# The S products of a row tile whole, in the second half of the down bank, and programs of their own for the end

## Chip, cores and metric

One core of a Trainium2 chip. The metric is the device time of one launch in microseconds (us). Engines: TensorE (PE; its weight loads PEld), VectorE (DVE), ScalarE (ACT), GpSimd (POOL), SyncE (SP, which issues the DMAs).

## What is computed

x has 4 batches of 2048 tokens of 256 features, fp32. Each token is normalised (xn). One branch is a linear attention with L2-normalised queries and keys, the other a feed-forward of 704 hidden features whose inputs, hidden values and weights are rounded to FP4 in blocks of 16:

```python
xn = _layernorm(x)
Q, K, V = xn @ Wq.T + bq, xn @ Wk.T + bk, xn @ Wv.T + bv
Q, K = l2_norm(Q) (over the tokens), l2_norm(K)
tailor_sum = 1 / (L + Q . (sum(K) + EPS))
s = xn + gamma * (sum(V) + Q @ (K^T V)) * tailor_sum
h = silu(fp4_linear(xn, w_gate)) * fp4_linear(xn, w_up)
g = silu(fp4_linear(h, w_down))
out = x + s * g
```

As Q and K are linear in xn, the kernel gets s of a token from one 256x256 matrix per batch: s = xn @ M. M comes from the Gram matrix of the batch's tokens, by small products, so it is known only after the whole batch was normalised.

## The kernel before, in words

The 8192 tokens are 32 pairs (PAIRS) of two row tiles (j = 0 and 1) of 128 tokens, 8 pairs a batch (PB). One pass p of `iteration` works on many pairs at once, each engine with its own program and its order written out by hand; semaphores (S[...]) count what is done. Passes 0 to 11 are written out, 12 to 27 are a loop of two rounds with 8 passes each (`drive`), 28 to 32 are written out again, then each engine has a tail.

In pass p: pair p+3 is normalised and p+2 rounded (x_..., VectorE L917 to L942, ScalarE, GpSimd L495 to L512), pair p has its gate and up products (`gate_up`, L1427, two column halves c into the banks GU[:, c, 0..1]), silu on ScalarE (L635) and their product h on VectorE (`h_mul`, L953); pair p-1 has its hidden values rounded (VectorE `h_scales` L960 to L967, `h_round` L990, L993, L1001, GpSimd L546, ScalarE L684); pair p-2 has its hidden values transposed (`hidden_transposes`, L1389, copied by ScalarE L642, L644) and multiplied by w_down (`down_product`, L1437, L1439, into DS[:, 0:256], "D's bank"), and ScalarE makes g of it (`g_out`, L671). Pair e = p-10 (LAGE) has its S product, xn @ M (`s_terms`, L1448: 6 matmuls, high and low parts in f16), which VectorE scales by unm and multiplies by g into y. GpSimd adds x for pair p-12 (L562) and SyncE writes it out and loads the x of a later one (xe).

A gate or up bank has 512 columns, of which 352 are used. The S product of a row tile stands as two halves of 128 columns in the spare columns of the up banks:

```python
def s_spare(c, m=1):
    return GU[:, c, m, CH:CH + P]
```

A pass begins on VectorE with `h_mul` (0, 0), right behind L967 of the pass before. `s_half` follows each gate-up product, `e_half` (L1012) reads it right behind `h_mul`, and for the bank's sake gate_up waits for y_d and h_mul for s_d. `s_place` says which row tile it is: in j = 1 the first one of pair p-10, in j = 0 the second one of pair p-11. Passes 10 to 31 have them in this way. `last_halves`: in one pass a batch (step i = FIRST, j = 0) both halves stand together, since the next matrix M is due then.

The attention's small products are asked of TensorE at places of a table (`ASKS`, (step i, j, place)), answered by VectorE (`ANSWERS`) and copied by ScalarE (`COPIES`), step by step: Gram matrix (L1497), turn (L1506), t1q and t1k (L1512, L1519), squares and norms (L1527), raw (L1534), tailor (L1544; VectorE L1060), product (L1551), top (L1556), high_low (L1561; VectorE L1093, L1095 write M). The last batch has its own tables (`..._END`).

The end: the 8 pairs of the last batch can only have their S product when M of that batch is there. They use whole banks of 256 columns (`s_product`, read by `e_mul`, L1024), and y has two places, so e_mul waits for o_d of GpSimd's add two pairs back. x of the last 7 pairs is loaded early into buffers that have become free (xend); GpSimd adds into these (L557).

## Time and profile before

| | us |
|---|---|
| three runs, median (lowest to highest) | 596.38 (595.67 to 596.96) |
| the profiled execution, its time | 597.39 |
| its span, first to last instruction | 595.3 |
| PE busy | 549.7 (92%) |
| DVE busy | 555.4 (93%) |
| ACT busy | 416.8 (70%) |
| POOL busy | 265.6 (45%) |

The mean granted clock of TensorE was 0.991 of full speed. All times of rows are of the one profiled execution and count from its first instruction. A row's duration reaches to the end of the instruction's drain; the next one of the same engine can start some 0.1 to 0.16 us before that, so what an instruction holds of its engine is the distance from its start to the next start. "x2" is two instructions merged into one row. In brackets stands the idle time ahead and what ended it.

### The profile page before, as it was taken

What the parts mean: (1) busy time and instruction counts of PE and PEld (TensorE: products, weight loads), DVE (VectorE), ACT (ScalarE), POOL (GpSimd) and SP (SyncE); (2) the same over time, 40 slices, a digit from 0 to 9 for tenths busy, and PEclk for the clock granted to TensorE, in tenths of its full rate; (3) what the DMA queues carried; (4) which work ended last, traced back from release to release, by engine and by line L of the source; (5) the groups of instructions that cost most, each with busy time, mean ns of one, the idle gap of its engine ahead of it and who ended that gap; (6) DMA issues with size and microseconds to landing.
All of it is one profiled execution on the core that took longest, in us unless ns stands there. A gap on an engine that the chain in (4) does not pass through costs nothing. (4 is left out here: it accounts for less than half of the span.)

```text
span 595.3 us, 15174 instructions
## 1 busy us (share of the span) xinstructions
PE 549.7 (92%) x4957; PEld 426.7 (72%) x4957; DVE 555.4 (93%) x1178; ACT 416.8 (70%) x901; POOL 265.6 (45%) x214
## 2 busy tenths in 40 slices
PE   0478999999999999999999989999999999999896
PEld 0355767777787777777887757778787777778775
DVE  7998999999999999999999998999999999977763
ACT  4979878877778777776777667877776776654421
POOL 7533333333433555355544453354743453423226
PEclk9999999999999999999999989999999999999999
DMA  8010000000011001111110111111011111132033
GB/s 251 18 37 19 19 20 19 19 20 19 19 37 37 19 3 55 55 55 55 55 55 2 54 58 55 56 55 54 2 55 55 55 37 37 36 103 95 0 124 143
DMA packets 17488, 29.14 MB, mean 49 GB/s; under 512 B 2688, under 2 KB 4864, under 8 KB 17408
## 3 DMA queue, kind: packets, MB, share of 16 engines
q1 hardware_dynamic: 17408, 28.13, 14.4%
q8 instruction: 44, 0.72, 0.5%
q14 instruction: 36, 0.29, 0.2%
HBM read 19.73 MB, written 8.39 MB: 47 GB/s over the span
## 5 line engine op out<-in xcount | busy, mean ns | idle before, releaser
L1427 PE MATMUL GU<-wgu,xqT 128*128 128x352 f16 x1536 | 252.8, 315 | 4.1 <-DVE h L953 2.6
L1427 PEld LDWEIGHTS GU<-wgu,xqT 128*128 128x128 f16 x1536 | 148.5, 99 | 78.3 <-issue 4.1
L546 POOL TENSOR_TENSOR ht<-h,hrr 128x1408 f32<-128x1408 f32 x32 | 82.9, 2590 | 80.5 <-DVE hrr L967 79.0
L635 ACT ACTIVATE sil<-GU,wkap 128x352 f32<-128x352 f32 x128 | 71.0, 555 | 60.0 <-PE GU L1427 59.1
L1437 PE MATMUL DS<-wdT,hqT 128*128 128x256 f16 x704 | 88.4, 275 | 1.9 <-ACT hqT L642 1.9
L953 DVE SCALAR_TENSOR_TENSOR h<-GU,wkap,sil 128x352 f32<-128x352 f32 x128 | 69.1, 540 | 11.9 <-ACT sil L635 8.0
L1001 DVE TENSOR_TENSOR hq<-hg,hs 128x704 f16<-128x704 f16 x128 | 79.1, 659 | 1.0
L1437 PEld LDWEIGHTS DS<-wdT,hqT 128*128 128x128 f16 x704 | 67.3, 99 | 12.5 <-ACT hqT L642 2.3
L505 POOL TENSOR_TENSOR xnat<-xs,xnat 128x510 f16<-128x510 f32 (+1 forms) x32 | 37.0, 1158 | 85.3 <-DVE hq L1001 72.9
L495 POOL TENSOR_TENSOR rs<-ve,half 128x2 f32<-128x2 f32 x32 | 22.9, 717 | 112.2 <-DVE ht L990 106.5
L671 ACT ACTIVATE gring<-DS,hun 128x256 f32<-128x256 f32 (+1 forms) x64 | 30.0, 468 | 44.9 <-issue 30.9
L642 ACT COPY hqT<-TR 128x768 f16<-128x768 f16 x64 | 51.0, 796 | 9.0 <-PE TR L1389 8.1
L990 DVE SCALAR_TENSOR_TENSOR ht<-hT,ht 128x1408 f32<-128x1408 f32 x32 | 51.8, 1620 | 1.5 <-ACT hT L684 1.5
L1439 PE MATMUL DS<-wdT,hqT 128*128 128x256 f16 x384 | 52.4, 273 | 0.0
L993 DVE SCALAR_TENSOR_TENSOR hg<-hT,ht 128x1408 f16<-128x1408 f32 x32 | 51.8, 1620 | 0.0
L960 DVE TENSOR_REDUCE ham<-h 128x88 f32<-128x1408 f32 x32 | 51.4, 1608 | 0.0
L1389 PE MATMUL TR<-id,hq 128*128 128x128 f16 x704 | 49.7, 219 | 0.0
L1448 PE MATMUL GU<-Mx,xnT 128*128 128x128 f16 (+1 forms) x552 | 47.7, 222 | 1.7 <-DVE Mx L1095 1.7
L1448 PEld LDWEIGHTS GU<-Mx,xnT 128*128 (+1 forms) x552 | 39.3, 98 | 12.1 <-issue 1.9
L512 POOL TENSOR_TENSOR xt<-xs,xrr 128x512 f32<-128x512 f32 x32 | 34.0, 1062 | 27.1 <-DVE hq L1001 25.2
L684 ACT ACTIVATE hT<-ht 128x1408 f32<-128x1408 f32 x32 | 43.9, 1371 | 1.8 <-POOL ht L546 1.3
L644 ACT COPY hqT<-TR 128x640 f16<-128x640 f16 x64 | 45.1, 705 | 0.0
(166 smaller groups left out, 975.5 us busy)
## 6 DMA issues: line engine op xcount, KB each, us to landing
xin<-in_L_attn_x SPq DMA_DIRECT2D x34, 256.0 KB, 2.9
xe<-in_L_attn_x SPq DMA_DIRECT2D x25, 256.0 KB, 2.8
out<-o SPq DMA_DIRECT2D x25, 256.0 KB, 2.0
algebra<-in_L_ffn_w_down SPq DMA_DIRECT2D x1, 704.0 KB, 6.2
gring<-in_L_ffn_w_up SPq DMA_DIRECT2D x1, 640.0 KB, 4.8
xs<-in_L_attn_x SPq DMA_DIRECT2D x2, 256.0 KB, 4.2
xt<-in_L_attn_x SPq DMA_DIRECT2D x2, 256.0 KB, 4.7
out<-xin SPq DMA_DIRECT2D x2, 256.0 KB, 4.1
```

Source lines behind the costliest of these rows:

```text
L546: g.tensor_tensor(paired(ht[:, 0:2 * I]), paired(h[:, q]), spread(hrr[:, q], 4 * CB), ALU.mult).then_inc(S["ht_d"], 1)
L635: a.activation(sil[:, c], GU[:, c, 0, 0:CH], ACT.Silu, scale=wkap[:, 0:1]).then_inc(S["sil_d"], 1)
L642: a.copy(hqT[:, j, 0:6], TR[:, j, 0:6 * P].rearrange("p (c m) -> p c m", m=P)).then_inc(S["hA_ev"], 1)
L953: v.scalar_tensor_tensor(h[:, k, (2 * j + c) * CH:(2 * j + c + 1) * CH], GU[:, c, 1, 0:CH], wkap[:, 0:1], sil[:, c], ALU.mult, ALU.mult).t ...
L960: v.tensor_reduce(per_block(ham[:, :]), paired_in_order(h[:, q]), AX.X, ALU.max, apply_absolute_value=True).then_inc(S["ham_d"], 1)
L990: v.scalar_tensor_tensor(ht[:, 0:2 * I], hT[:, 0:2 * I], CUT, ht[:, 0:2 * I], ALU.max, ALU.subtract).then_inc(S["hw_d"], 1)
L993: v.scalar_tensor_tensor(hg[:, 0:2 * I], hT[:, 0:2 * I], CUT, ht[:, 0:2 * I], ALU.max, ALU.subtract).then_inc(S["hg_d"], 1)
L1001: v.tensor_tensor(paired(hq[:, q, j, at:at + I]), paired(hg[:, j * I:(j + 1) * I]), spread(scales[:, q, j * HB:(j + 1) * HB], HB), ALU.mul ...
L1427: last = t.matmul(GU[:, c, m, 0:CH], xqT[:, k, j, 2 * a_ + kc], wgu[:, b_, kc, 2 * m + c], start=(z == 0 and kc == 0), stop=(z == 2 and kc ...
L1437: t.matmul(DS[:, 0:D], hqT[:, j, z], wdT[:, z], start=(z == 0), stop=False)
L1439: last = t.matmul(DS[:, 0:D], hqT[:, j, LOCH + z], wdT[:, NCH + z], start=False, stop=(z == LOCH))
L1448: last = t.matmul(bank, slot[:, j, 2 * a_ + kc], Mb[:, b_, kc, columns], start=(i == 0 and kc == 0), stop=(i == 2 and kc == KD - 1))
```

## The change

- The S product of a row tile (except `last_halves` and the last pair of halves, in the tail) is one of 256 columns (`s_wide`) into DS[:, 256:512], the second half of D's bank. TensorE makes it at the start of `down_product`, which first waits until the last one is read (y_d).
- VectorE reads it in one instruction (`e_wide`) that also waits for g_d of the same pass and row tile, that is, until ScalarE has read D of it. For j = 0 it stands ahead of the first instruction of `h_round`, for j = 1 behind the last of `h_round` and ahead of `h_scales` (L960). The waits of gate_up on y_d and of h_mul on s_d go (but in one place a batch).
- Answers: gram1 moves behind the first half of the layernorm statistics, high_low ahead of L917.
- t1k uses the symmetry of the Gram matrix: 6 products of 128 columns in place of 4 of 256; ScalarE writes a doubled copy of a part of wkT once (`wkT_twice`).
- The end: pass 32 on TensorE and VectorE is a program of its own, which mixes product, top and high_low with the S products of pairs 21 to 23, the down products and the rounding. Each y of the last 8 pairs has its own place (in h, ht, y[:, 0]; the last one in G, in PSUM), and e_mul waits for no add of the pairs before but in one place. x of pair 24 is loaded into h. GpSimd waits for the last rounding ahead of the add of pair 22. The last pair's add is on VectorE in two halves (`o_last`), each with a DMA of its own.

Cut to its core (left out: tables of semaphores, the same edits in SyncE's and GpSimd's programs, ScalarE's copy):

```diff
-        ANSWERS = {(0, 0, 3): "gram0", (1, 0, 1): "gram1", (1, 1, 0): "turn", (2, 1, 0): "squares",
-                   (3, 0, 0): "norms", (4, 0, 0): "tailor", (4, 0, 3): "scale", (4, 1, 0): "product", (4, 1, 2): "top", (5, 0, 2): "high_low"}
+        ANSWERS = {(0, 0, 3): "gram0", (1, 0, 5): "gram1", (1, 1, 0): "turn", (2, 1, 0): "squares",
+                   (3, 0, 0): "norms", (4, 0, 0): "tailor", (4, 0, 3): "scale", (4, 1, 0): "product", (4, 1, 2): "top", (5, 0, 4): "high_low"}
...
-                    (1, 1, 1): "t1k", (2, 0, 0): "norms", (2, 0, 2): "raw", (2, 1, 1): "tailor", (3, 0, 0): "product",
-                    (3, 0, 1): "top", (3, 0, 3): "high_low"}
+                    (1, 1, 1): "t1k", (2, 0, 0): "norms", (2, 0, 2): "raw", (2, 1, 1): "tailor"}
...
+        def y_place(e):
+            n = e - (PAIRS - PB) + 1
+            if n < 4:
+                return h[:, n // 2, n % 2 * 2 * D:(n % 2 + 1) * 2 * D]
+            return ht[:, (n - 4) * 2 * D:(n - 3) * 2 * D] if n < 7 else y[:, 0]
         def end_row(p):
-            return xend[p - LAGO - (PAIRS - ENDS)]
+            n = p - LAGO - (PAIRS - ENDS)
+            return h[:, 0, 0:2 * D] if n < 0 else xend[n]
...
+                if isinstance(p, int) and p == PAIRS:
+                    sp.wait_ge(S["ht_d"], PAIRS - 1)
+                    sp.dma_start(h[:, 0, 0:2 * D], rows(xf, PAIRS - PB)).then_inc(S["x_mid_in"], 16)
...
+                    if isinstance(e, int) and e == PAIRS - LAGE:
+                        pool.wait_ge(S["hloq"], 2 * PAIRS)
+                    y_ = y_place(e) if isinstance(e, int) and e >= PAIRS - PB else y[:, ko]
...
-                if s_beside(p, j, False):
-                    wait(dve, "s_d", n - 4 * LAGE - 1 + (c == 0 and last_halves(j, i)))
+                if c == 0 and last_halves(j, i) and s_beside(p, j, False):
+                    wait(dve, "s_d", n - 4 * LAGE)
...
+            def e_wide(p, k, j):
+                e, q, row = s_place(p, k, j)
+                wait(dve, "s_d", 4 * e + 2 * row + 2)
+                wait(dve, "g_d", 2 * (p - LAGH) + j + 1)
+                if row == 0:
+                    wait(dve, "o_d", e - 1)
+                v.scalar_tensor_tensor(y[:, q, row * D:(row + 1) * D], DS[:, D:2 * D], unm[:, 0:1],
+                                       ring(gring, e, GRING)[:, row], ALU.mult, ALU.mult).then_inc(S["y_d"], 2)
...
+            def y_last(j):
+                return G[:, j * D:(j + 1) * D]
+            def o_last(j):
+                own = slice(j * D, (j + 1) * D)
+                dve.wait_ge(S["xend_in"], 16 * ENDS)
+                dve.wait_ge(S["y_d"], 4 * PAIRS - 2 + 2 * j)
+                v.tensor_tensor(xend[ENDS - 1][:, own], y_last(j), xend[ENDS - 1][:, own], ALU.add).then_inc(S["last_d"], 1)
...
+                elif e == PAIRS - 1:
+                    to = y_last(j)
+                else:
+                    if j == 0 and e < PAIRS - 2:
+                        dve.wait_ge(S["ht_d"], PAIRS)
+                    if j == 0 and e == PAIRS - 2:
+                        dve.wait_ge(S["o_d"], PAIRS + 1 - LAGE)
+                    to = y_place(e)[:, j * D:(j + 1) * D]
+                v.scalar_tensor_tensor(to, GU[:, j, k, 0:D], unm[:, int(e >= PAIRS - PB):int(e >= PAIRS - PB) + 1],
...
-                if s_beside(p, 0, tail):
-                    e_half(p, k, 0, 0, last_halves(0, i))
                 if s_beside(p, 0, tail) and last_halves(0, i):
+                    e_half(p, k, 0, 0, True)
...
-                if s_beside(p, 0, tail) and not last_halves(0, i):
-                    e_half(p, k, 0, 1)
...
+                if s_beside(p, 0, tail) and not last_halves(0, i):
+                    e_wide(p, k, 0)
                 if on["mb"]:
...
                     h_mul(p, k, 1, 0, i)
-                if s_beside(p, 1, tail):
-                    e_half(p, k, 1, 0)
...
                     h_mul(p, k, 1, 1, i)
-                if s_beside(p, 1, tail):
-                    e_half(p, k, 1, 1)
                 attention(1, 1)
                 if on["mb"]:
                     h_round(p, k, 3)
+                if s_beside(p, 1, tail):
+                    e_wide(p, k, 1)
...
+                p, k, b = PAIRS, PAIRS % 2, BATCHES - 1
+                e_half(p, k, 0, 0)
+                answer(b, "product")
+                parts(p, k, 0)
+                parts(p, k, 1)
+                e_half(p, k, 0, 1)
+                answer(b, "top")
+                answer(b, "high_low")
+                e_mul(p, k, 0)
+                e_mul(p, k, 1)
+                parts(p, k, 2)
+                h_round(p, k, 0)
+                e_mul(p + 1, 1 - k, 0)
+                h_round(p, k, 1)
+                e_mul(p + 1, 1 - k, 1)
+                h_round(p, k, 2)
+                e_mul(p + 2, k, 0)
+                e_mul(p + 2, k, 1)
+                h_round(p, k, 3)
+                for p in range(PAIRS + 3, PAIRS + LAGE):
                     for j in range(2):
                         e_mul(p, p % 2, j)
...
+                        if p == PAIRS + LAGE - 1:
+                            o_last(j)
...
-                if s_on:
-                    wait(pe, "y_d", n - 4 * LAGE - 3 + ((i, j, c) == (FIRST, 1, 0)))
+                if s_on and (i, j, c) == (FIRST, 1, 0):
+                    wait(pe, "y_d", 4 * (p - LAGE))
...
+            def s_wide(p, k, j, b, i):
+                e, _, row = s_place(p, k, j)
+                if (i, j) == (FIRST, 1):
+                    wait(pe, "mats", b + 1)
+                s_terms(DS[:, D:2 * D], e, row, slice(0, D), 2)
+            def down_product(p, k, j, s_on=False, b=0, i=-1):
                 n = 2 * (p - LAGH) + j
+                if s_beside(p, 0, False) if j else s_beside(p - 1, 1, False):
+                    wait(pe, "y_d", 4 * (p - LAGE) - 2 + 2 * j)
                 wait(pe, "hA_ev", n + 1)
                 wait(pe, "hB_ev", n + 1)
                 wait(pe, "g_d", n)
+                if s_on:
+                    s_wide(p, k, j, b, i)
...
                     for m in range(KD):
-                        for k in range(KD):
-                            last = t.matmul(G[:, m * D:(m + 1) * D], wkT[:, k, m * P:(m + 1) * P], Gs[:, k],
-                                            start=(k == 0), stop=(k == KD - 1))
+                        own = slice(m * P, (m + 1) * P)
+                        t.matmul(G[:, m * D:m * D + P], wkT[:, 0, own], Gs[:, 0, 0:P], start=True, stop=False)
+                        t.matmul(G[:, m * D:m * D + P], wkT_twice[:, own], Gs[:, 1, 0:P], start=False, stop=True)
+                        last = t.matmul(G[:, m * D + P:(m + 1) * D], wkT[:, 1, own], Gs[:, 1, P:D], start=True, stop=True)
...
-                    if s_on:
+                    if s_on and last_halves(j, i):
...
-                    if s_on and not last_halves(j, i):
-                        s_half(p, k, j, 1, b, i)
...
-                        down_product(p, k, j)
+                        down_product(p, k, j, s_on and not last_halves(j, i), b, i)
...
+                p, k = PAIRS, PAIRS % 2
+                s_half(p, k, 0, 0, last, PB - 5)
+                for c in range(2):
+                    hidden_transposes(p, k, 0, c, False)
+                ask(last, "product")
+                s_half(p, k, 0, 1, last, PB - 5)
+                down_product(p, k, 0)
+                ask(last, "top")
+                s_product(p, k, 0, last, False)
+                for c in range(2):
+                    hidden_transposes(p, k, 1, c, False)
+                ask(last, "high_low")
+                s_product(p, k, 1, last, False)
+                s_pair(PAIRS + 1 - LAGE)
+                down_product(p, k, 1)
+                p, k, first = PAIRS + 1, (PAIRS + 1) % 2, PAIRS + 2 - LAGE
```

## Rows read from the trace of the kernel before

**Rows 1.** Busy us and instructions of PE, PEld, DVE, ACT, POOL in the loop.

```profile
210.00:350.00 140.00, 137.61 (x1286) 107.33 (x1283) 137.99 (x299) 102.47 (x219) 70.05 (x51) 1.00 0.14 47
```

**Rows 2.** Timeline of VectorE, pass 19; start us, duration us, engine, line, operation.

```profile
339.42 0.70 DVE L967 RECIPROCAL hrr<-hss 128x88 f32<-128x88 f32 x1
...
343.29 1.28 DVE L933 SCALAR_TENSOR_TENSOR xt<-xT,xt 128x512 f32<-128x512 f32 x1
...
351.90 0.34 DVE L1012 SCALAR_TENSOR_TENSOR y<-GU,unm,gring 128x128 f32<-128x128 f32 x1
352.16 1.60 DVE L1001 TENSOR_TENSOR hq<-hg,hs 128x704 f16<-128x704 f16 x2
353.69 1.60 DVE L960 TENSOR_REDUCE ham<-h 128x88 f32<-128x1408 f32 x1
```

**Rows 3.** Timeline of VectorE, pass 4 (no S product yet) and pass 10.

```profile
94.79 0.70 DVE L967 RECIPROCAL hrr<-hss 128x88 f32<-128x88 f32 x1
...
98.03 0.68 DVE L933 SCALAR_TENSOR_TENSOR xt<-xT,xt 128x512 f32<-128x512 f32 x1
...
105.29 0.58 DVE L953 SCALAR_TENSOR_TENSOR h<-GU,wkap,sil 128x352 f32<-128x352 f32 x1
...
107.34 1.61 DVE L960 TENSOR_REDUCE ham<-h 128x88 f32<-128x1408 f32 x1
...
200.51 0.58 DVE L953 SCALAR_TENSOR_TENSOR h<-GU,wkap,sil 128x352 f32<-128x352 f32 x1
...
202.57 1.61 DVE L960 TENSOR_REDUCE ham<-h 128x88 f32<-128x1408 f32 x1
```

**Rows 4.** Timeline of GpSimd in the stretch of rows 2.

```profile
342.75 1.28 POOL L562 TENSOR_TENSOR o<-y,xe 128x512 f32<-128x512 f32 x1
...
351.80 1.16 POOL L505 TENSOR_TENSOR xnat<-xs,xnat 128x510 f32 x1 [1.24 <-DVE hq L1001]
```

**Rows 5.** Timeline of TensorE, a half of S in pass 31 and the last ten S products.

```profile
542.22 0.50 PE L1448 MATMUL GU<-Mx,xnT 128*128 128x128 f16 x6
542.55 0.78 PE L1389 MATMUL TR<-id,hq 128*128 128x128 f16 x11
...
584.12 6.71 PE L1448 MATMUL GU<-Mx_end,xnT 128*128 128x256 f16 x60
```

**Rows 6.** Groups by form; busy us, mean ns of one, idle before.

```profile
L1012 DVE SCALAR_TENSOR_TENSOR y<-GU,unm,gring 128x128 f32<-128x128 f32 x88 | 29.9, 342 | 0.0
...
L1519 PE MATMUL G<-algebra,wkT 128*128 128x256 f32 x32 | 7.6, 381 | 0.0
```

**Rows 7.** Timeline of VectorE, readers of whole S products in the end.

```profile
577.56 0.88 DVE L1024 SCALAR_TENSOR_TENSOR y<-GU,unm,gring 128x256 f32<-128x256 f32 x2 [0.35 <-POOL o L562]
581.14 1.07 DVE L1024 SCALAR_TENSOR_TENSOR y<-GU,unm,gring 128x256 f32<-128x256 f32 x2 [2.70 <-POOL o L562]
```

**Rows 8.** Timeline of ScalarE, g_out of the second row tile, passes 30 and 31.

```profile
540.68 0.47 ACT L671 ACTIVATE gring<-DS,hun 128x256 f32<-128x256 f32 x1 [3.10 <-PE DS L1439]
...
558.02 0.48 ACT L671 ACTIVATE gring<-DS,hun 128x256 f32<-128x256 f32 x1 [3.00 <-PE DS L1439]
```

**Rows 9.** Timeline of VectorE, passes 30 and 31.

```profile
539.19 1.61 DVE L960 TENSOR_REDUCE ham<-h 128x88 f32<-128x1408 f32 x1
...
557.22 1.62 DVE L960 TENSOR_REDUCE ham<-h 128x88 f32<-128x1408 f32 x1
558.75 0.34 DVE L1060 SCALAR_TENSOR_TENSOR den<-G,inv,width 128x1 f32<-128x1 f32 x2
```

**Rows 10.** Timeline of TensorE, the last batch's norms, product and top.

```profile
543.16 1.00 PE L1527 MATMUL G<-ones,wqkv 128*128 128x1 f32 x8
...
559.14 1.99 PE L1551 MATMUL G<-wqkv,algebra 128*128 128x256 f32 x8 [0.26 <-DVE den L1060]
...
562.92 0.38 PE L1556 MATMUL G<-mtop,ones 128*128 128x1 f32 x2 [1.45 <-DVE mtop L1080]
```

**Rows 11.** Timeline of GpSimd, the last add of the output.

```profile
591.50 1.26 POOL L557 TENSOR_TENSOR xT<-y,xT 128x512 f32<-128x512 f32 x1
```

More of the change, by code:

```diff
@@ L271, in build @@
                     (0, 1, 0): "gram1_0", (0, 1, 1): "gram1_1", (1, 0, 0): "turn", (1, 0, 2): "t1q",
-                    (1, 1, 1): "t1k", (2, 0, 0): "norms", (2, 0, 2): "raw", (2, 1, 1): "tailor", (3, 0, 0): "product",
-                    (3, 0, 1): "top", (3, 0, 3): "high_low"}
+                    (1, 1, 1): "t1k", (2, 0, 0): "norms", (2, 0, 2): "raw", (2, 1, 1): "tailor"}
         ANSWERS_END = {(0, 0, 2): "gram0", (0, 1, 2): "gram1", (1, 0, 1): "turn", (1, 1, 2): "squares",
-                       (2, 0, 1): "norms", (2, 1, 2): "tailor", (2, 1, 3): "scale", (3, 0, 0): "product",
-                       (3, 0, 1): "top", (3, 0, 4): "high_low"}
+                       (2, 0, 1): "norms", (2, 1, 2): "tailor", (2, 1, 3): "scale"}
         COPIES_END = {(1, 1, 0): "t1q", (2, 1, 0): "raw"}
@@ L303, in drive @@
                     iteration(b * PB + i, i % 2, b + later, step)
-            for p in range((BATCHES - 1) * PB + 4, PAIRS + 1):
+            for p in range((BATCHES - 1) * PB + 4, PAIRS if tail else PAIRS + 1):
                 iteration(p, p % 2, *batch_step(p))
@@ L442, in iteration @@
                     e = p - LAGO
-                    wait(sp, "o_d", e + 1)
+                    if not (isinstance(e, int) and e == PAIRS - 1):
+                        wait(sp, "o_d", e + 1)
                     ko = (k + LAGO) % 2
+                    if isinstance(e, int) and e == PAIRS - 1:
+                        for j in range(2):
+                            own = slice(j * D, (j + 1) * D)
+                            sp.wait_ge(S["last_d"], j + 1)
+                            sp.dma_start(rows(of, e)[:, own], end_row(p)[:, own]).then_inc(S[f"out_d{ko}"], 16)
+                        return
                     sp.dma_start(rows(of, e), end_row(p) if at_end(p) else o[:, ko]).then_inc(S[f"out_d{ko}"], 16)
-                if on["e"] and not (isinstance(p, int) and p - LAGE >= PAIRS - ENDS):
+                if isinstance(p, int) and p == PAIRS:
+                    sp.wait_ge(S["ht_d"], PAIRS - 1)
+                    sp.dma_start(h[:, 0, 0:2 * D], rows(xf, PAIRS - PB)).then_inc(S["x_mid_in"], 16)
+                if on["e"] and not (isinstance(p, int) and p - LAGE >= PAIRS - PB):
                     ke = (k + LAGE) % 2
@@ L551, in iteration @@
                     g.tensor_tensor(inv[:, :], nrm[:, :], half[:, :], ALU.pow).then_inc(S["inv_d"], 1)
-                if on["o"]:
+                if on["o"] and not (isinstance(p, int) and p - LAGO == PAIRS - 1):
                     e, ko = p - LAGO, (k + LAGO) % 2
                     wait(pool, "y_d", 4 * e + 4)
+                    if isinstance(e, int) and e == PAIRS - LAGE:
+                        pool.wait_ge(S["hloq"], 2 * PAIRS)
+                    y_ = y_place(e) if isinstance(e, int) and e >= PAIRS - PB else y[:, ko]
                     if at_end(p):
-                        pool.wait_ge(S["xend_in"], 16 * ENDS)
-                        g.tensor_tensor(end_row(p), y[:, ko], end_row(p), ALU.add).then_inc(S["o_d"], 1)
+                        pool.wait_ge(*((S["x_mid_in"], 16) if e == PAIRS - PB else (S["xend_in"], 16 * ENDS)))
+                        g.tensor_tensor(end_row(p), y_, end_row(p), ALU.add).then_inc(S["o_d"], 1)
                     else:
@@ L561, in iteration @@
                         wait(pool, f"out_d{ko}", 8 * (e - ko) + 16)
-                        g.tensor_tensor(o[:, ko], y[:, ko], xe[:, ko], ALU.add).then_inc(S["o_d"], 1)
+                        g.tensor_tensor(o[:, ko], y_, xe[:, ko], ALU.add).then_inc(S["o_d"], 1)
                 if isinstance(p, int) and p == 0:
@@ L611, in copy @@
                     act.wait_ge(S["a_tr"], i + 1)
+                    if i:
+                        a.activation(wkT_twice[:, :], G[:, D:2 * D], ACT.Copy, scale=2.0)
                     a.copy((wqT, wkT)[i][:, :, :], matrices).then_inc(S["a_ev"], 1)
@@ L1020, in e_mul @@
                 wait(dve, "g_d", n + 1)
[L1021 to L1024 removed]
+                if e < PAIRS - PB:
+                    if j == 0:
+                        wait(dve, "o_d", e - 1)
+                    to = y[:, e % 2, j * D:(j + 1) * D]
+                elif e == PAIRS - 1:
[7 more added lines that the diff above has]
+                v.scalar_tensor_tensor(to, GU[:, j, k, 0:D], unm[:, int(e >= PAIRS - PB):int(e >= PAIRS - PB) + 1],
                                        ring(gring, e, GRING)[:, j], ALU.mult, ALU.mult).then_inc(S["y_d"], 2)
@@ L1244, in iteration @@
                     x_front(p + 1, 1 - k)
+                attention(0, 5)
                 if on["xf"]:
@@ L1310, in tail @@
             def tail():
-                for p in range(PAIRS + 1, PAIRS + LAGE):
+                p, k, b = PAIRS, PAIRS % 2, BATCHES - 1
[18 more added lines that the diff above has]
+                for p in range(PAIRS + 3, PAIRS + LAGE):
                     for j in range(2):
                         e_mul(p, p % 2, j)
+                        if p == PAIRS + LAGE - 1:
+                            o_last(j)
             drive(dve, iteration, tail)
```

21 lines of the change are left out of this document (9 added, 12 removed).

## The prediction, made before the changed kernel ran

> **What bounds the kernel now.** I read the busy time by stretch first, then the timelines of VectorE and GpSimd through one pass of the loop beside each other, then the same places in passes that have no S product yet, and last the timelines of the last batch. In the loop TensorE and VectorE both show over 98% busy [rows 1]. Which of the two leads is seen in the VectorE timeline: of the pass in [rows 2] each instruction starts where the one before it has drained, and the pass takes as long as their sum. So an edit is worth in the loop what it takes off VectorE's row or puts on it. But two of its instructions there are longer than their work. L933 took 1.28 us and takes 0.68 where GpSimd is idle [rows 2, 3]; it started at 343.29, GpSimd's output add ran from 342.75 to 344.03 [rows 4], and L933 ended 0.54 after that, which is its own work less a little. The two L1001 of the second row tile took 1.60 together and began after L505 of GpSimd had; that one ends at 352.96 [rows 4], and 0.75 later they are done. All of these read two tensors of SBUF on VectorE while GpSimd reads SBUF too. The trace has the test without S: with no half ahead of the two L1001 the way from the last L953 to L960 is 2.05 (105.29 to 107.34), and with a half in it 2.06 (200.51 to 202.57) [rows 3]. The half there costs nothing. It fills a wait for GpSimd.
>
> **The change part by part.** All sums in us of VectorE's row unless said.
>
> *S on TensorE.* 6 matmuls of 256 columns for 12 of 128. The last 60 wide ones take 6.71 with the drain of the last, 0.65 for six; a half is 0.50 long with its drain and holds TensorE from 542.22 to 542.55, 0.33, so 0.66 for two [rows 5]. Zero: a column costs the same either way.
>
> *The readers.* A half is 0.34 long [rows 6] and holds the row for 0.26: 351.90 to 352.16 [rows 2]. A wide one is 0.48 and two of them 0.88 [rows 7], so 0.40 each. Bounds for e_wide: 0.34 and 0.48; I take 0.40, as it is the same instruction. Per pass, four halves (1.04) go and two wide ones (0.80) come. Now place by place. (a) The two halves of j=0 lie ahead of L933. Without them L933 would come 0.51 earlier, at about +3.36 from the start of L967 instead of +3.87 (339.42 to 343.29) [rows 2], and +3.24 in a pass without S (94.79 to 98.03) [rows 3]; GpSimd's add starts at +3.33 (342.75) [rows 4]. Either L933 loses and waits for the add as now: gain 0. Or it slips in ahead, and L936 waits for the add instead: gain about 0.18. (b) The first half of j=1: 0.26 gained. (c) The second: 0, as shown. (d) Both wide ones stand where nothing of GpSimd is waited for (ahead of L990 and of L960): 0.80 lost. Sum +0.54 a pass, less 0 to 0.18.
>
> There are 44 row tiles with S beside the gate and up products, 88 halves [rows 6], so passes 10 to 31. Ten passes are of the kind just worked out (12, 13, 15, 17, 19, 21, 23, 25, 27, 28): 5.4. Four (14, 16, 22, 24) have answers of the attention ahead of L933 or another GpSimd step ahead of the add, so it is not held fully now; there the lost halves give back between 0 and 0.51, I take half: +0.28 each, 1.1. Two (11, 20) have L933 free: 0.80 less 0.77, 0.1 together. Three (10, 18, 26) have only one wide product: 0.40 less 0.26, 0.4 together. That is 7.0. Less half of the possible 0.18 in six passes, 0.5. At the handing over to the last batch, where TensorE leads, some 0.5 of VectorE's delay falls into TensorE's slack. **6.0 reaches the last batch**; ends 4.5 (e_wide at 0.34, all six slip) and 8 (e_wide at 0.48).
>
> *New waits.* down_product now waits for the reader of the half bank beside D, and e_wide waits for g_d. Ahead of down_product the reader is done at least some 0.3 before, in the loop; what a miss would delay is a gate-up product with over 1 us in hand. Zero. e_wide of j=0 is behind g_out, which ends some 1 us earlier. Zero. But e_wide of j=1 is behind g_out of j=1, and behind it are queued L960 and all answers of VectorE. In the loop g_out is done 4 us before. In the last batch it is not: L671 runs from 540.68 to 541.15 where L960 started at 539.19 already, and from 558.02 to 558.50 where L960 started at 557.22 [rows 8, 9].
>
> *t1k.* 4 products of 256 columns (8 records, 1.78 a set; mean 0.381 a record [rows 6]) become 6 of 128: 768 columns for 1024, 1.33. In the loop it is TensorE's alone and hidden under VectorE's row: 0. In the last batch -0.45. The doubled copy of wkT is one ACT instruction once, at most 0.4, beside the weights' transposes; 0.
>
> *Last batch, up to the product.* The turn waits for an answer that stands behind e_wide: +0.7 by the same shift, and 0.33 of S work comes later in the pass: with t1k +0.6 at the end of pass 30, TensorE ends its D product at 541.0 (540.43, which is 0.25 ahead of L671 [rows 8], and 0.6). From there: 0.25 to g_out, 0.47, 0.40 e_wide, 1.53 L960, 1.28 squares, 0.2 of semaphores: 545.1 for the norms, which started at 543.16 [rows 10]: +1.9. Pass 31 the same way: D ends at 560.05, then 0.72, 0.40, 1.53, 0.37 for the tailor's L1060 (558.75 before [rows 9]), 0.1: the product starts at 563.2 in place of 559.14 [rows 10]. **+4.1.** Ends: 1.5 (an answer covered) and 5.
>
> *The end.* From the product to the end it was 595.3 - 559.1 = 36.2. VectorE waited for y places, 2.70 at once [rows 7], and TensorE for the top, 1.45 [rows 10]. After: product 1.8, half 0.3, D 1.9, top 0.3, S 0.65, transposes 0.6, high_low 0.5, three S 1.95, D 1.9 (9.9); 16 S tiles 10.4, two sets of transposes 1.2, two D 3.7, 1.2 for y and hq, 0.8 for ACT's hqT, 0.3 of semaphores (17.6); TensorE ends 27.6 after the product starts. Then the last y 0.5, its add on VectorE 0.35 in place of GpSimd's 1.26, 0.1, and as now 2.5 from the end of the last add, 592.76 [rows 11], to the end. 31.1: **-5.1.** Ends -1.5 (GpSimd's adds, 1.27 each and all behind the last rounding, set the end) and -8.
>
> Sum: 6.0 + 4.1 - 5.1 = +5.0. The profiled execution took 597.4, span 595.3: 602.4 for it. It stands 1.0 above the median shown, 596.4, so **601.4**. A measurement here can tell about 0.2%, 1.2 us, from no change.
>
> **Rivals.** *The halves come off in full, faster.* The Trainium skill, VectorE: DVE Perf Modes, the section on the TRN2 errata, has a fixed cost for each instruction, 120 cycles from PSUM, so that small tiles pay it per tile; an estimate from its table is 0.52 for two halves and 0.39 for a whole. By that rule the trace agrees on the price of one, and every merged tile would gain 0.12. As a mechanism here: GpSimd's add and L505 would have to let VectorE go earlier, as it happens if L933 slips in and L936 is not held. Each pass for which that holds is 0.77 cheaper than I have it; from about 7 of 20 on (5.0 / 0.77) the kernel is no longer slower. All: 41 tiles by 0.12 is -4.9, with +4.1 and -5.1: 590.5. Against it: 2.05 beside 2.06 [rows 3]. Chance 0.18.
>
> *GpSimd ends last.* Its adds wait for the last rounding and then follow at 1.27; if they, not TensorE's S, set the end, -5.1 becomes -1.5: 605. For it: nine of them in a row. Chance 0.10.
>
> *g_out is not in the way.* If L960 and the answers had more slack than I read, +4.1 falls to about 0: 597.3. Chance 0.12.
>
> **How the numbers follow.** My forecast has 0.60, its own range 599 to 604.5. The range goes down to 595 and up to 605: it leaves out most of the first rival and a little above. Faster (under 595.2) 0.19; same 0.07, from the edge of the third rival; slower 0.74.
>
> **What would show it.** Right: two L1024-like readers of 0.48 a pass in place of four; L933 still 1.1 to 1.28 long or L936 1.6; the way from L953 to L960 longer by 0.40, 2.7 in the loop, and a pass without attention work longer by about 0.5 (L967 to L960, 339.42 to 353.69, is 14.27 here [rows 2]). In the last batch VectorE idle ahead of e_wide with ACT L671 as releaser, and TensorE idle ahead of the norms and of the product; at the end a row of S products with hardly a gap. Wrong: L933 at 0.68 and passes no longer than before, or the last S product followed by a queue of adds on GpSimd.

## The result, and the profile of the changed kernel

| us | before | after |
|---|---|---|
| time, median of 4 runs each on one chip | 596.12 (595.67 to 596.96) | 602.76 (600.65 to 604.53) |
| ratio to before, 95% interval | | 1.0104, 1.0083 to 1.0126 |
| the profiled execution, its span | 595.3 | 600.6 |
| PE, DVE, POOL busy | 549.7, 555.4, 265.6 | 548.7, 560.0, 247.5 |

The kernel is 1.0% slower, 6.6 us by the medians and 5.3 between the two profiled spans; 601.4 and a range of 595 to 605 were forecast. The sum came out near partly by luck: the loop costs 2.4 less than forecast, the last batch 1.8 more and the end gives 0.8 less, and these errors nearly cancel. To see it I split the span at two places that both kernels have: the start of the reciprocal that ends a pass on VectorE (L967 before, L992 after), and the start of TensorE's product of the last batch. After minus before: 0.06 at the end of pass 9, 3.68 at the end of pass 28, 9.62 at the product (568.76 against 559.14 of [rows 10]), 5.3 at the last instruction. So:

| us | forecast | measured |
|---|---|---|
| loop, passes 10 to 28 | +6.0 | +3.6 |
| last batch up to the product | +4.1 | +5.9 |
| product to the end | -5.1 | -4.3 |

**The loop.** VectorE's timeline of the changed kernel in pass 19, the pass of [rows 2]:

```profile
341.31 0.70 DVE L992 RECIPROCAL hrr<-hss 128x88 f32<-128x88 f32 x1
...
344.58 0.68 DVE L958 SCALAR_TENSOR_TENSOR xt<-xT,xt 128x512 f32<-128x512 f32 x1
345.30 1.65 DVE L961 SCALAR_TENSOR_TENSOR xg<-xT,xt 128x512 f16<-128x512 f32 x1
...
347.41 0.47 DVE L1049 SCALAR_TENSOR_TENSOR y<-DS,unm,gring 128x256 f32<-128x256 f32 x1
347.80 1.61 DVE L1015 SCALAR_TENSOR_TENSOR ht<-hT,ht 128x1408 f32<-128x1408 f32 x1
...
353.19 0.58 DVE L978 SCALAR_TENSOR_TENSOR h<-GU,wkap,sil 128x352 f32<-128x352 f32 x1
353.69 1.85 DVE L1026 TENSOR_TENSOR hq<-hg,hs 128x704 f16<-128x704 f16 x2
355.47 0.47 DVE L1049 SCALAR_TENSOR_TENSOR y<-DS,unm,gring 128x256 f32<-128x256 f32 x1
355.86 1.60 DVE L985 TENSOR_REDUCE ham<-h 128x88 f32<-128x1408 f32 x1
```

and GpSimd's beside it:

```profile
344.64 1.76 POOL L584 TENSOR_TENSOR o<-y,xe 128x512 f32<-128x512 f32 x1
...
353.58 1.15 POOL L523 TENSOR_TENSOR xnat<-xs,xnat 128x510 f32 x1 [2.78 <-DVE hq L1026]
```

L958 and L961 are the L933 and L936 of before, L1026 is L1001, L985 is L960, and GpSimd's L584 and L523 are L562 and L505. e_wide (L1049) is 0.47 long and holds the row for 0.39 in both places: the 0.40 of the working. The two L1026 take 1.85 in place of 1.60, since the half that used to fill their wait for L523 is gone: from the last L978 to e_wide it is 2.28, as from the last L953 before (351.41, just ahead of the half at 351.90) to L960 (353.69) in [rows 2]. So a reader's removal there brought nothing and e_wide behind it costs 0.39. At the other place, with both halves of the first row tile gone from ahead of it, L958 now does slip in 0.06 ahead of GpSimd's add; the add then takes 1.76 in place of 1.28, and L961 pays, with 1.65 in place of 0.69. From L992 to L1015 it is 6.49, 0.39 of it e_wide; before, from L967 to L990 (339.42 to 345.75), it was 6.33. So the slip gives 0.23 here, more than my 0.18.

**The last batch.** VectorE's waits from 520 to 570 (us in all, times, longest), and three of the five, in passes 30 and 31:

```profile
DVE y L1049 <- ACT gring L695: 7.9, 5, 2.5
```

```profile
545.60 0.48 DVE L1049 SCALAR_TENSOR_TENSOR y<-DS,unm,gring 128x256 f32<-128x256 f32 x1 [2.20 <-ACT gring L695]
556.69 0.48 DVE L1049 SCALAR_TENSOR_TENSOR y<-DS,unm,gring 128x256 f32<-128x256 f32 x1 [2.53 <-ACT gring L695]
566.45 0.48 DVE L1049 SCALAR_TENSOR_TENSOR y<-DS,unm,gring 128x256 f32<-128x256 f32 x1 [1.83 <-ACT gring L695]
```

The first and the third are e_wide of the second row tile, and theirs is the wait that was forecast. The one at 556.69 is the first row tile's, where none was forecast; run 2 below shows that it doesn't count. TensorE's timeline shows what the waits do, and the windows beside it (us, then busy time and instructions of PE, PEld, DVE, ACT, POOL; the third column from the right is the granted clock) something that was not:

```profile
548.95 1.05 PE L1617 MATMUL G<-ones,wqkv 128*128 128x1 f32 x8 [1.71 <-DVE algebra L1104]
549.87 2.51 PE L1504 MATMUL GU<-wgu,xqT 128*128 128x352 f16 x12
552.17 1.49 PE L1538 MATMUL DS<-Mx,xnT 128*128 128x256 f16 x6
...
555.84 1.89 PE L1624 MATMUL G<-algebra,wkT 128*128 128x256 f32 x8
...
568.76 1.56 PE L1641 MATMUL G<-wqkv,algebra 128*128 128x256 f32 x6 [2.13 <-DVE den L1117]
...
591.28 5.40 PE L1538 MATMUL GU<-Mx_end,xnT 128*128 128x256 f16 x48
```

```profile
545.00:550.00 5.00, 3.29 (x31) 2.57 (x30) 4.37 (x10) 2.23 (x4) 0.17 (x1) 1.00 0.01 2
550.00:556.00 6.00, 6.00 (x37) 4.26 (x35) 1.56 (x7) 2.54 (x6) 4.61 (x3) 0.72 0.22 70
```

Behind the idle 1.71 ahead of the norms the granted clock is 0.72 on average over six us, a part of them at the lower of its two levels (1.2 in place of 2.4 GHz). The gate-up, S and D products behind the norms take 5.97, from 549.87 to 555.84.

**The end.** From the product to the last instruction it is 31.8, where it was 36.1. The last S products are a row without gaps from 591.28 to 596.68. GpSimd's last add is done at 597.29, VectorE's (L1060) at 598.07; their rows:

```profile
597.06 0.48 DVE L1081 SCALAR_TENSOR_TENSOR G<-GU,unm,gring 128x256 f32<-128x256 f32 x1
597.65 0.42 DVE L1060 TENSOR_TENSOR xT<-G,xT 128x256 f32<-128x256 f32 x1
```

```profile
596.03 1.26 POOL L579 TENSOR_TENSOR xt<-y,xt 128x512 f32<-128x512 f32 x1
```

### The profile page after: what moved, and what is told of

The parts are those of the page before. It is cut to its first block, busy times and chain, and to the rows that moved or that the text cites. A ratio compares the mean times of both kernels' runs of the same rounds, so it can differ in the third digit from the quotient of the medians.

```text
span 600.6 us, 14473 instructions
## 1 busy us (share of the span) xinstructions
PE 548.7 (91%) x4727; PEld 421.9 (70%) x4727; DVE 560.0 (93%) x1139; ACT 411.6 (69%) x902; POOL 247.5 (41%) x213
## 4 chain that ended last, share of the span: by engine, by line
PE 58%; DVE 23%; issue 12%; ACT 3%; POOL 2%; DMA 1%; DVEq 0%; SPq 0%; POOLq 0%; ACTq 0%
PE GU L1504 25%; PE DS L1527 8%; PE TR L1465 4%; PE DS L1529 4%; PE DS L1538 3%; PE G L1583 3%; DVE hg L1018 3%; DVE hq L1026 2%; DVE ham L985 2%; DVE h L978 2%; PE GU L1538 2%; PE TR L1481 2%; PE TR L1405 2%; DVE xq L967 1%; DVE ht L1015 1%
## 5 line engine op out<-in xcount | busy, mean ns | idle before, releaser
L1026 DVE TENSOR_TENSOR hq<-hg,hs 128x704 f16<-128x704 f16 x128 | 83.9, 696 | 0.8
L523 POOL TENSOR_TENSOR xnat<-xs,xnat 128x510 f16<-128x510 f32 (+1 forms) x32 | 36.9, 1156 | 101.0 <-DVE hq L1026 85.3
L978 DVE SCALAR_TENSOR_TENSOR h<-GU,wkap,sil 128x352 f32<-128x352 f32 x128 | 68.5, 535 | 9.9 <-ACT sil L659 7.4
L1527 PEld LDWEIGHTS DS<-wdT,hqT 128*128 128x128 f16 x704 | 68.5, 98 | 9.5 <-ACT hqT L666 0.9
L1015 DVE SCALAR_TENSOR_TENSOR ht<-hT,ht 128x1408 f32<-128x1408 f32 x32 | 51.7, 1614 | 0.0
L985 DVE TENSOR_REDUCE ham<-h 128x88 f32<-128x1408 f32 x32 | 51.4, 1606 | 0.0
L1465 PEld LDWEIGHTS TR<-id,hq 128*128 128x128 f16 x704 | 44.0, 98 | 9.6 <-DVE hq L1026 3.2
L1529 PEld LDWEIGHTS DS<-wdT,hqT 128*128 128x128 f16 x384 | 37.6, 98 | 4.3
```

Of the source, the lines that this page charges most:

```text
L978: v.scalar_tensor_tensor(h[:, k, (2 * j + c) * CH:(2 * j + c + 1) * CH], GU[:, c, 1, 0:CH], wkap[:, 0:1], sil[:, c], ALU.mult, ALU.mult).t ...
L985: v.tensor_reduce(per_block(ham[:, :]), paired_in_order(h[:, q]), AX.X, ALU.max, apply_absolute_value=True).then_inc(S["ham_d"], 1)
L1015: v.scalar_tensor_tensor(ht[:, 0:2 * I], hT[:, 0:2 * I], CUT, ht[:, 0:2 * I], ALU.max, ALU.subtract).then_inc(S["hw_d"], 1)
L1026: v.tensor_tensor(paired(hq[:, q, j, at:at + I]), paired(hg[:, j * I:(j + 1) * I]), spread(scales[:, q, j * HB:(j + 1) * HB], HB), ALU.mul ...
L1465: last = t.transpose(TR[:, bank, zz * P:(zz + 1) * P], hq[:, q, j, z * P:(z + 1) * P], id16[:, :])
L1527: t.matmul(DS[:, 0:D], hqT[:, j, z], wdT[:, z], start=(z == 0), stop=False)
```

## The experiments

Theory: VectorE's row sets the loop, readers of S cost there only outside the waits for GpSimd, in the last batch e_wide behind g_out is in the way, and the new end is worth its 4 to 5. Times are medians, beside 596.3 for the kernel before on the same chips in the first six runs, 597.2 and 597.8 in the others, so there ratios are compared.

### 1. Halves in the passes, everything else of the change

```diff
-                if s_beside(p, 0, tail) and not last_halves(0, i):
-                    e_wide(p, k, 0)
...
+                if s_beside(p, 1, tail):
+                    e_half(p, k, 1, 0)
...
-                        down_product(p, k, j, s_on and not last_halves(j, i), b, i)
+                        down_product(p, k, j)
```

> The changed kernel with the S products of passes 10 to 31 as halves again (their old places and waits), and the new t1k, answers' places and end kept. My theory says that readers and the wait behind g_out cost 3.6 us in the loop and 6 in the last batch, and that the end gains 4.4 to 5: then this is 590.5 to 592, 5 under the kernel before and 11 under the changed one. If the new end is worth nothing by itself (GpSimd's adds end last), it is at the kernel before, 595.5 to 597. If it is the answers' new places that cost the time in the loop, it stays within 2 us of the changed kernel, above 598.

592.5 (592.06 to 592.92), ratio 0.9933 (0.9909 to 0.9957), 0.5 above what was expected. The new end alone is worth 3.8 us, t1k and the answers' places with it; GpSimd's adds don't take it back. From pass 9 to pass 28 its trace gains 0.23 on the kernel before. The product starts at 558.06, with TensorE's wait 0.26 long as in [rows 10], and the span ends 32.5 behind it. So all of the loss is in the readers and their waits.

### 2. The late reader

```diff
-                if s_beside(p, 1, tail):
+                if s_beside(p, 1, tail) and not (isinstance(p, int) and p >= PAIRS - 3):
                     e_wide(p, k, 1)
...
                     h_scales(p, k, 2)
+                if s_beside(p, 1, tail) and isinstance(p, int) and p >= PAIRS - 3:
+                    e_wide(p, k, 1)
```

> The changed kernel with e_wide of the second row tile moved behind L985, the answers and the rest of h_scales in passes 29 to 31 only. My theory (the wait for g_out is in the way of L985 and the answers) says 5 to 6 us less, 596.5 to 598: no idle time of VectorE ahead of L985, TensorE's wait ahead of the norms back to about 0.3, no stretch with a granted clock of 0.72 there, and the product some 5 us earlier. If g_out is not in the way, it is within 1 us of the changed kernel, 602 to 603.5. If only the wait goes and the clock falls elsewhere instead, 598.5 to 600.

596.2 (595.54 to 596.83), ratio 0.9996 (0.9984 to 1.0007): 6.6 less than the changed kernel, a little more than expected. In its TensorE timeline the norms have no wait, the product neither, and the window behind is at full clock:

```profile
546.88 1.00 PE L1619 MATMUL G<-ones,wqkv 128*128 128x1 f32 x8
547.74 1.95 PE L1506 MATMUL GU<-wgu,xqT 128*128 128x352 f16 x12
549.53 0.82 PE L1540 MATMUL DS<-Mx,xnT 128*128 128x256 f16 x6
...
552.04 1.89 PE L1626 MATMUL G<-algebra,wkT 128*128 128x256 f32 x8
...
562.68 1.97 PE L1643 MATMUL G<-wqkv,algebra 128*128 128x256 f32 x8
```

```profile
550.00:556.00 6.00, 6.00 (x49) 4.88 (x47) 3.04 (x5) 2.99 (x8) 1.74 (x2) 1.00 0.29 90
```

The same gate-up, S and D products take 4.30 here (547.74 to 552.04), where they took 5.97: 1.7 of the 6.6 is the clock. The first row tile's e_wide still waits for g_out, 1.07 in pass 30 and 1.42 in pass 31, and TensorE has no wait behind it: that one is covered. The place of one instruction on VectorE, in three passes, was worth as much as the whole change had cost. The loop of this run is still 3.7 behind that of the kernel before.

### 3 and 4. One half's reader doubled, in the kernel before

```diff
+                if j == 1 and c == 0:
+                    v.scalar_tensor_tensor(spare_y[:, :], s_spare(c), unm[:, 0:1],
+                                           ring(gring, e, GRING)[:, row, c * P:(c + 1) * P], ALU.mult, ALU.mult)
                 v.scalar_tensor_tensor(y[:, q, row * D + c * P:row * D + (c + 1) * P],
```

and the same with `c == 1`.

> The kernel before with the reader of the first half of the second row tile issued twice, its copy written to a place of its own. VectorE's row theory: that place fills no wait, so it holds 0.26 more in each pass, the step from its start to the next instruction goes from 0.26 to 0.52 in passes 10 to 28, and the time is 3.5 to 5.5 us longer, 600 to 601.5. If TensorE led in the loop, less than 1 us.

> The kernel before with the reader of the second half of the second row tile issued twice. My theory: that half fills the wait of L1001 for GpSimd's L505, so the way from the last L953 to L960 stays at 2.06 to 2.3 in passes 12 to 28 and the time is 0 to 1.2 us longer, 596 to 597.5. If each reader costs its 0.26 wherever it stands (the rival in which halves come off in full), 3.5 to 5.5 us longer, as the run with the first half doubled.

600.35 (599.9 to 601.05), ratio 1.0067 (1.0043 to 1.0092), with the first one doubled; 597.05 (595.44 to 597.77), ratio 1.0004 (0.9989 to 1.0020), with the second. It is the same instruction on the same bytes, and it costs 0.24 to 0.27 in 16 of the passes 10 to 28 (4.1 in sum) in one place and at most 0.03 in the same passes in the other. VectorE's timeline with the second doubled:

```profile
352.28 0.34 DVE L1014 SCALAR_TENSOR_TENSOR spare_y<-GU,unm,gring 128x128 f32<-128x128 f32 x1
352.54 0.34 DVE L1016 SCALAR_TENSOR_TENSOR y<-GU,unm,gring 128x128 f32<-128x128 f32 x1
352.79 1.34 DVE L1002 TENSOR_TENSOR hq<-hg,hs 128x704 f16<-128x704 f16 x2
354.06 1.61 DVE L961 TENSOR_REDUCE ham<-h 128x88 f32<-128x1408 f32 x1
```

The extra reader is paid by the next row: 1.34 with two readers ahead of it, 1.60 with one [rows 2], 1.85 with none (above). GpSimd's L506 there runs from 352.17 to 353.32, and VectorE is through 0.74 after it whatever stands ahead. That settles the rival in which halves come off in full. By the Trainium skill, SBUF — State Buffer, section Who interferes with whom, a VectorE instruction with two inputs in SBUF contends with a GpSimd instruction that reads SBUF, and the order of issue decides which of the two is blocked. The trace agrees on both orders: L933 1.28 when GpSimd is first, GpSimd's add 1.76 in place of 1.28 when L958 is.

### 5. The early reader

Run 2, and the reader of the second row tile moved in the other passes too:

```diff
                     h_mul(p, k, 1, 1, i)
+                if s_beside(p, 1, tail) and not (isinstance(p, int) and p >= PAIRS - 3):
+                    e_wide(p, k, 1)
                 attention(1, 1)
                 if on["mb"]:
                     h_round(p, k, 3)
-                if s_beside(p, 1, tail) and not (isinstance(p, int) and p >= PAIRS - 3):
-                    e_wide(p, k, 1)
```

> The kernel of the run with the late reader, and in passes 11 to 28 e_wide of the second row tile also moved, to right behind the last h_mul, ahead of the two L1026 that wait for GpSimd's L523. My theory (a reader of whole tiles costs only where no wait for GpSimd lies) says that the way from that h_mul to L985 goes from 2.67 back to 2.28 in the passes in which L523 runs then, about 15 of them: 0.40 each, 6 us less than with the late reader alone, 590 to 592. If VectorE's delay was already partly in TensorE's slack, so that TensorE leads once VectorE is shorter: 592 to 594.5. If the place doesn't matter (each reader costs its 0.40 anywhere): as the late reader, 595.5 to 597.

589.9 (589.71 to 591.67), ratio 0.9889 (0.9858 to 0.9920): 6.3 less than run 2. Per pass it is 0.35 to 0.40 in 17 of the 19, where I had counted on 15, and in passes 16 and 24 0.31 and 0.36 are given back. The same two instructions in its trace, in the order that costs nothing:

```profile
350.15 0.58 DVE L978 SCALAR_TENSOR_TENSOR h<-GU,wkap,sil 128x352 f32<-128x352 f32 x1
350.64 0.47 DVE L1049 SCALAR_TENSOR_TENSOR y<-DS,unm,gring 128x256 f32<-128x256 f32 x1
351.04 1.47 DVE L1026 TENSOR_TENSOR hq<-hg,hs 128x704 f16<-128x704 f16 x2
352.43 1.61 DVE L985 TENSOR_REDUCE ham<-h 128x88 f32<-128x1408 f32 x1
```

### 6. Halves for the first row tile, whole tiles for the second: the fastest version

```diff
                 if on["m"]:
                     h_mul(p, k, 0, 1, i)
+                if s_beside(p, 0, tail) and not last_halves(0, i):
+                    e_half(p, k, 0, 1)
...
-                if s_beside(p, 0, tail) and not last_halves(0, i):
-                    e_wide(p, k, 0)
...
-                        down_product(p, k, j, s_on and not last_halves(j, i), b, i)
+                        down_product(p, k, j, s_on and j == 1, b, i)
```

> The kernel before's halves for the first row tile (both lie in the wait of L958 for GpSimd's add), whole tiles in D's bank with the early reader for the second one (late in passes 29 to 31), the new t1k and the new end. My theory: against the kernel with halves everywhere and the new end (592.5) each pass loses one reader outside a wait, 0.26 in some 17 passes, so 587.5 to 590 if VectorE leads all along, and 3 us under the run with early whole readers for both row tiles. If TensorE leads from there on, 590 to 592. If merging gains nothing at all, 592.5.

588.0 (587.44 to 588.81), ratio 0.9848 (0.9820 to 0.9877), below both kernels. Against run 1 the pass is 0.24 to 0.28 shorter in 16 of 19, one reader outside a wait; against run 5 it is 1.9 less in place of my 3, in part because in the six passes with the slip it gives e_wide of the first row tile back 0.26 of its 0.39: they are only 0.13 to 0.16 shorter than in run 5, passes 17, 25 and 28 0.39 to 0.40. Its L958 is 1.27 long again, with two halves ahead of it.

### 7 and 8. Which pass of the last batch

The late reader in passes 29 and 30 only (`p in (PAIRS - 3, PAIRS - 2)` in the two conditions of run 2), and in pass 31 only (`p == PAIRS - 1`).

> The changed kernel with the late reader in passes 29 and 30 only; pass 31 keeps e_wide ahead of L985, behind g_out. The late reader in all three gave 596.2. Theory: half of the last batch's loss is the granted clock of 0.72 behind TensorE's wait ahead of the norms. Then the norms come without a wait, that dip is gone, and what is left is pass 31's wait for g_out, 1.5 to 2.5: 597.7 to 598.7. If the clock has no part, pass 31's share of the loss is 3.2 and it is 599.2 to 600. If a wait for g_out in pass 31 is covered, 596 to 597.

> The changed kernel with the late reader in pass 31 only; the norms come late as in the changed kernel. Theory: TensorE waits about 1.7 ahead of the norms, and the granted clock is lower in some 6 us behind it again; together 3.5 to 4.5 over the 596.2 of the run with the late reader in all three passes: 599.7 to 600.7. If the clock doesn't fall this time (the dip had another cause than that wait), 598 to 598.8. Together with the run of passes 29 and 30 the two losses should add to the 6.6 between the changed kernel and the late reader.

598.33, ratio 1.0023 (1.0009 to 1.0038), and 600.07, ratio 1.0046 (1.0029 to 1.0063). By ratios against run 2 pass 31's wait costs 0.27%, 1.6 us, as expected, and the norms' wait 0.50%, 3.0 us, below the 3.5 to 4.5 expected. The sum, 4.6, is short of the 6.5 that run 2 gained by its ratio. The single runs of the second kernel tell why in part: the ten reach from 598.32 to 601.29, and the three at 598.32, 598.35 and 598.68 had a mean granted clock of 0.996 or 0.997, the three above 600.7 one of 0.991 to 0.994. The profiled one is the slowest, and the clock in its windows fell further and for longer than in the changed kernel's:

```profile
545.00:550.00 5.00, 3.29 (x27) 2.72 (x26) 4.82 (x13) 1.84 (x3) 0.94 (x1) 0.85 0.00 2
550.00:556.00 6.00, 6.00 (x29) 3.74 (x28) 1.02 (x3) 2.54 (x6) 3.84 (x3) 0.56 0.24 87
```

The traces add up where the times don't. Counted from the end of pass 28, the norms start at 32.95 in run 2 and at 35.60 in run 8 and in the changed kernel: the wait itself is worth 2.65. From the norms to the product it is 15.80 in run 2 and 19.17 in run 8, which has no further wait on this way: 3.4 more, all of it the clock, which the two windows above put at the same, 0.15 of 5 us and 0.44 of 6. In run 7, with the norms on time and 1.00 in both windows, it is 18.09: 2.3 for pass 31's wait alone. The changed kernel has 2.65, these 2.3 and 1.7 of clock, together the 6.7 by which its product comes later than in run 2. So in the traces the norms' wait costs 2.65 by itself, and the clock behind it 1.7 or 3.4 more, or nothing: run 11 below has the same 1.71 idle ahead of the norms and 1.00 behind it.

### 9 and 10. GpSimd's output add cut short, before and after

```diff
-                        g.tensor_tensor(o[:, ko], y[:, ko], xe[:, ko], ALU.add).then_inc(S["o_d"], 1)
+                        g.tensor_tensor(o[:, ko, 0:16], y[:, ko, 0:16], xe[:, ko, 0:16], ALU.add).then_inc(S["o_d"], 1)
```

> The kernel before with GpSimd's output add in passes 12 to 31 cut to 16 of 512 columns (the other columns of those outputs stay zero; a fill of o in pass 6 added). Theory: it is GpSimd's read of SBUF that stretches L934 to 1.28. Then L934 is 0.68 in every pass, VectorE's row is 0.6 shorter in some 12 passes, and as TensorE has only some 0.3 of idle time a pass the time falls by 3 to 6, 590.5 to 593.5. If L934 is held by something else, such as the S halves' bank, it stays at 1.28 and the time at 595.5 to 597.

> The changed kernel with the same cut of the add (same columns left zero). Theory: L961 goes from 1.65 to 0.69, and now nothing hides the halves that were removed: the loop of this kernel is within 1 us of the loop of the kernel before with the same cut, in place of 3.6 behind it, and what stays is last batch and end, +1.6: 0.5 to 3 us over that run. If the adds have nothing to do with what the halves were worth, it stays 5 to 6.5 over it.

These kernels write 16 of the 512 columns of the outputs and leave the others at zero; they are there for their time alone. 591.3, ratio 0.9896 (0.9874 to 0.9919), as expected: L933 (L935 here) is 0.68 in every pass of the loop, and four of the six passes where it had been 1.28 (13, 19, 21 and 27) are each 0.6 shorter. The other two are not: pass 15 is 0.38 shorter and pass 23 0.56 longer. I had expected 0.6 in some twelve. The second came to 598.4, ratio 1.0014 (0.9996 to 1.0033), 1.2% over run 9 and not 0.5 to 3 us. VectorE's waits of that run from 205 to 505 show, beside the 2.4 at the loop's back edge, waits that are not in the changed kernel's trace:

```profile
DVE y L1051 <- ACT gring L697: 3.4, 5, 1.0
DVE h L980 <- issue: 2.4, 1, 2.4
DVE h L980 <- ACT sil L661: 1.8, 5, 0.5
```

In an ordinary pass my theory holds: from the end of pass 18 to that of 19 it is 15.63 here and 15.55 in run 9, 0.08 apart, where the two full kernels differ by 0.28 there (16.43 and 16.15). In the whole loop it is 4.3 over run 9. Five passes (12, 15, 20, 22, 23) have the waits of 3.4 in sum: there VectorE, now that it is held up less, comes to e_wide of the first row tile before ScalarE has finished g_out. But together these passes are only 1.55 longer than in run 9, so the waits are not the whole account. Passes 17, 25 and 28 are 0.48, 0.44 and 0.71 longer without one, the first two with waits for sil (0.16 and 0.55 in pass 17, 0.20 there in run 9). Behind the loop this run loses another 2.3 on run 9, last batch and end together, beside the 1.6 that was expected.

### 11. The same, with that reader one place later

```diff
-                if s_beside(p, 0, tail) and not last_halves(0, i):
-                    e_wide(p, k, 0)
                 if on["mb"]:
                     h_round(p, k, 0)
+                if s_beside(p, 0, tail) and not last_halves(0, i):
+                    e_wide(p, k, 0)
```

> The changed kernel with the short add (598.4) and e_wide of the first row tile moved one place back, behind L1017 (1.53 later). The trace of the short add has five waits of e_wide of the first row tile for ScalarE's g_out in the loop, 0.18 to 0.97, 3.3 in sum, just what this kernel is behind the kernel before with the short add there. Theory: with the reader 1.53 later these waits go, and the loop is within 1 us of that kernel's: 594.5 to 596. If TensorE or something else held those passes, the time goes elsewhere and it stays at 597.5 to 599.

597.3 (595.42 to 599.16), ratio 1.0003 (0.9989 to 1.0017). The interval overlaps that of run 10 (1.0014), so by time this is inconclusive, and the 3 us did not come: it is still 1.1% over run 9. (The profiled execution is the fastest of ten here, 595.42, and the slowest of ten in run 10, 599.82, so the spans of the two traces say less than their passes.) In the loop the waits for g_out are gone, and these stand in their place.

```profile
DVE h L980 <- ACT sil L661: 4.7, 9, 2.5
DVE ht L1017 <- ACT hT L710: 1.2, 2, 0.6
```

In the 4.7 is the wait at the loop's back edge, 2.5, which run 10 shows under issue. The other 2.2, and hT's 1.2, are short waits for ScalarE, sil behind TensorE's gate and up products. Between the ends of passes 11 and 27 this run loses 1.3 on run 9, run 10 loses 3.2. So by the traces 1.9 of the 3.2 came back with the waits for g_out, and 1.3 stays. What holds ScalarE and TensorE in those passes was not traced further, and stays open.

## Why the prediction came out as it did

- **What bounds the loop.** Right: run 3's price of 0.25 a pass for one added reader is VectorE's row.
- **(b), (c), (d), prices and places.** Right: first half of the second row tile 0.26 (run 3: 0.24 to 0.27), its second half 0 (run 4), e_wide 0.39 (0.40 taken; run 5: 0.35 to 0.40 in 17 passes).
- **(a), the slip.** I gave it half of 0.18 a pass in six passes, 0.5. It happened in every pass in which L933 had been 1.28, and for 0.26, going by the passes' length. The six (13, 15, 19, 21, 23, 27) are 0.27 to 0.29 longer each, not 0.54: 1.1 less than forecast.
- **How many ordinary passes.** I took ten; with pass 12 held 0.14. Only 17, 25 and 28 cost about the 0.54 that I had for all ten (0.51 to 0.53), and there something else is at work as well: L933 had been 0.84 to 0.94 and L958 is 1.44 to 1.47.
- **Passes with answers, and the back edge.** Forecast +0.28 for each of 14, 16, 22, 24; measured 0.34, -0.06, 0.37, -0.05. Pass 20, across the loop's back edge, is 0.77 shorter than before. VectorE stands idle there for 2.77 and 0.39 before and for 2.46 after, while TensorE is busy throughout (9.00 of 9.00 from 355 to 364 in both traces), so its wait isn't its own row, and part of its delay falls away. I had this effect only at the handing over to the last batch. This 0.77 is good to some 0.3 only: the four traces with the changed kernel's loop (changed kernel, runs 2, 7, 8) have 18.20 to 18.50 for the pass, and the kernel before, 18.99, has a granted clock of 0.72 from 350 to 356, where run 4 has 1.00 and 18.71. Together these terms make 3.6 out of 6.0.
- **The last batch.** Mechanism and place right for the second row tile (runs 2, 7, 8), the size too small: 5.9 for 4.1. The step that was too small is "Pass 31 the same way". The norms came 2.1 later than the loop's part, 1.9 forecast. From the norms to the product it was 3.8 more, where the forecast has 2.1 for the wait alone. Run 7, at full clock, has just these 2.1 (18.09 against 15.98 before). The other 1.7 is the clock: 0.72 behind the wait, and 5.97 for products that take 4.30 at 1.00. A wait of TensorE was priced at its length alone.
- **e_wide of the first row tile.** "Zero" was right for the time, but not its reason: g_out does not end ahead of it in the last batch. It waited 1.07 and 2.53 there, and run 2, which keeps these waits at 1.07 and 1.42, shows them covered.
- **t1k.** The set of the last batch starts at 540.77 and what follows it at 542.16, 1.39 in place of 1.78: -0.4 for my -0.45.
- **The end.** -4.3 for -5.1; run 1 has 3.8 for it in time. Of the 4.3 the clock of one execution is 1.6: runs 3 and 4 have the old end with 1.00 in the windows behind the same 1.45 wait for top, and take 34.6 in both, where the kernel before took 36.1 with 0.72. At full clock the new end is worth 2.7. The forecast took the 36.2 as they stood. TensorE ends 27.9 after the product (27.6 forecast). The last add ends 1.4 behind that, for 0.95 forecast; the add of the first half (596.72) stands between the two last readers. From there it is 2.5 to the end, as forecast.
- **Rivals.** GpSimd ends last: no, its last add ends at 597.29, ahead of VectorE's 598.07. g_out not in the way: no, run 2. Halves off in full: no, runs 3 and 4. Yet run 6 shows how near it was: it is 15 us faster than the changed kernel, by the late reader in the last batch (6.6, run 2), the early one in the loop (6.3, run 5) and the halves in the first row tile (1.9).

## What to carry to other kernels

Before an instruction is merged, moved or removed on the engine that leads, look at what the next one waits for: doubled in place it tells in one run whether its time is paid or hidden, and the same reader was worth 0.25 in one place and 0.00 in another here. In front of an instruction that has to wait for another engine a short one is free as long as it fits into that wait (runs 4 and 5), so the new reader belongs there. And of a new wait ask who is queued behind it: here three answers to the engine that sets the end, which cost 6.6 us and were got back by moving one line for three passes.

## What the runs showed of the hardware

- A slow clock comes behind a wait of TensorE, but not in every execution. Behind 1.71 idle ahead of the norms the changed kernel's trace has 0.72 over 6 us and run 8's 0.85 over 5 and 0.56 over 6, while run 11's, with the same 1.71, has 1.00; behind the 2.13 idle ahead of the product the changed kernel's window has 1.00. Behind the same 1.45 ahead of top the kernel before has 0.72 and runs 3 and 4 have 1.00. What decides it the traces don't show. The spread of the times fits this: run 2, without a wait from the norms to the product, spreads over 1.3 us in ten executions, run 8 over 3.0, and the kernel before over 3.3 in the 25 beside run 8. This is the window of the kernel before behind its 1.45 wait for top [rows 10]:

```profile
562.00:568.00 6.00, 4.63 (x27) 3.71 (x28) 3.31 (x10) 2.21 (x6) 4.31 (x3) 0.72 0.30 105
```

  Part of what the new end brings is that this wait is no longer there: run 1 has 1.00 from 520 to 585.
- When VectorE is ahead of GpSimd by 0.06, GpSimd's instruction is the one that is stretched (1.76 for 1.28), and the VectorE instruction behind it waits for all of it (1.65 for 0.69). The wait is then 0.96 long and not 0.60, and that is why two readers less ahead of it, 0.51 by their price, gave only about half of that (0.23 to 0.26).
